# A transformer layer on one core: a new order for the last attention group and the batch norm sums, and a shorter form of its last two tiles

## The reference, cut to what matters

```python
h = layernorm(x)
q, k, v = relu(h @ Wq + bq), relu(h @ Wk + bk), relu(h @ Wv + bv)
y = softmax(q @ k.T / sqrt(512) - 1e4 * causal) @ v
x1 = x + layernorm(relu(y @ Wo + bo))
h2 = layernorm(x1)
for side in (out, in_):                     # two sides, each with its own weights
    xc = einsum('ngf,gf->ng', h2.reshape(n, 128, 4), conv_w) + conv_b
    mean, var = over all 8192 rows of xc    # batch norm: needs every row
    xa = gelu((xc - mean) * rsqrt(var + eps) * gamma + beta)
    score[side] = softmax(xa @ lin_w.T + lin_b)
# out: (h2 @ W) kept where score is in its top 32 of 512 columns, times the score
# in:  (h2 kept where score is in its top 32, times the score) @ W
return x1 + layernorm(out_branch + in_branch + bias)
```

## Time and profile before

| what | value |
|---|---|
| median of 3 runs | 2086.85 us (2084.85 to 2088.97) |
| the profiled execution, its own time | 2083.91 us |
| its span, first to last instruction | 2082.1 us |
| TensorE (PE) busy | 2008.6 us, 96% |
| VectorE (DVE) busy | 1529.4 us, 73% |
| ScalarE (ACT) busy | 1104.9 us, 53% |
| GpSimd (POOL) busy | 1096.3 us, 53% |
| mean granted TensorE clock | 0.992 of full |

### The profile page before, as it was taken

One profiled execution on the slowest core, in us unless ns is written; L12 is line 12 of the kernel. 1 busy time (PEld: TensorE's weight loads), 2 busy tenths in 40 slices (PEclk: granted clock), 3 DMA queues, 4 the chain that ended last, 5 costly groups with the idle time before them and its releaser, 6 DMA issues. The chain is left out here.

```text
span 2082.1 us, 30834 instructions
## 1 busy us (share of the span) xinstructions
PE 2008.6 (96%) x9402; PEld 940.9 (45%) x9402; DVE 1529.4 (73%) x3344; ACT 1104.9 (53%) x2270; POOL 1096.3 (53%) x1302
## 2 busy tenths in 40 slices
PE   8999999999999999999999999988999999999997
PEld 4444444444444444444444444443444444444443
DVE  6676554677645568655557764578999999999998
ACT  5444333254333344442334433325888888888886
POOL 2243322363332254423234431324899999999998
PEclk9999999999999999999999999989999999999999
DMA  5344343354242424434334332451222222222322
GB/s 184 79 91 106 75 96 73 103 115 117 69 107 65 110 69 117 104 83 99 76 95 111 93 87 60 115 152 41 69 94 98 86 87 97 87 90 93 102 77 71
DMA packets 301593, 194.85 MB, mean 94 GB/s; under 512 B 223858, under 2 KB 241394, under 8 KB 301428
## 3 DMA queue, kind: packets, MB, share of 16 engines
q1 hardware_dynamic: 301428, 192.88, 34.8%
HBM read 82.69 MB, written 58.72 MB: 68 GB/s over the span
## 5 line engine op out<-in xcount | busy, mean ns | idle before, releaser
L616 PE MATMUL psum<-hT,w_hi 128*128 128x512 f16 (+1 forms) x1544 | 458.4, 379 | 0.0
L616 PE MATMUL psum<-kT,qT 128*128 128x512 f16 (+3 forms) x1920 | 363.4, 347 | 1.5 <-DVE kT L1112 1.5
L616 PE MATMUL psum<-v,pT 128*128 128x512 f16 x1632 | 362.5, 379 | 0.6 <-DMA pT<-phl 0.6
L616 PE MATMUL psum<-hT,w_lo 128*128 128x512 f16 (+1 forms) x772 | 292.3, 379 | 0.0
L616 PEld LDWEIGHTS psum<-kT,qT 128*128 128x128 f16 x1920 | 180.9, 98 | 184.3 <-issue 2.9
L868 ACT ACTIVATE sS<-sS,nm 128x128 f32<-128x128 f32 (+7 forms) x64 | 76.9, 1202 | 348.0 <-DVE nm L1149 347.8
L857 ACT ACTIVATE raw<-psum,bqkv_s 128x512 f32<-128x512 f32 x192 | 131.2, 683 | 218.8 <-PE psum L616 216.8
L616 PEld LDWEIGHTS psum<-v,pT 128*128 128x128 f16 x1632 | 159.7, 98 | 193.0 <-issue 1.1
L1373 DVE MAX8 c<-cut 128x8 f32<-128x512 f32 x384 | 244.2, 676 | 0.0
L616 PEld LDWEIGHTS psum<-hT,w_hi 128*128 128x128 f16 x1544 | 151.5, 98 | 176.1 <-DVE w_lo L1086 0.2
L1498 POOL TENSOR_SCALAR ve<-mv 128x1 f32<-128x1 f32 x64 | 21.9, 342 | 347.1 <-DVE mv L1175 346.2
(11 more groups left out here) (159 smaller groups left out, 3819.1 us busy)
## 6 DMA issues: line engine op xcount, KB each, us to landing
xg<-x SPq DMA_DIRECT2D x64, 256.0 KB, 5.3
xr<-x SPq DMA_DIRECT2D x64, 256.0 KB, 2.9
x_scratch<-xr SPq DMA_DIRECT2D x64, 256.0 KB, 2.1
h_scratch<-hb SPq DMA_DIRECT2D x64, 256.0 KB, 3.0
h<-h_scratch SPq DMA_DIRECT2D x64, 256.0 KB, 2.7
x<-x_scratch SPq DMA_DIRECT2D x64, 256.0 KB, 2.9
out<-zn SPq DMA_DIRECT2D x59, 256.0 KB, 2.0
xc_scratch<-dsq SPq DMA_DIRECT2D x64, 128.0 KB, 2.0
```

The lines of the kernel that those rows point to most:

```text
L616: mm = nc.tensor.matmul(outp, stat(a), mov(c), start=(n == 0 and k == 0), stop=(n == total - 1 and k == 2))
```

## The change

It touches what lies after the scores of tile 63. Four parts:

1. The lists of all engines for the last four tiles are written out by hand in another order, and the main loops end one half step earlier (PREP + 4).
2. For the tiles 62 and 63 (`SHORT` = 62 on), VectorE makes the sum x + scale*o in one step without the layer norm's shift (`residual_in`); it takes statistics of that, and convolves rows that are centred but not yet scaled (`unscaled_convolution`), the scale coming in with the pilot's subtraction (`scaled_deviations`). ScalarE adds the shift afterwards, for the copy of x1 that is stored (`residual_out`). `normed` and GpSimd's `residual` fall away for these two tiles; h2 for the store is made later, by `second_rows`.
3. TensorE's sums of tiles 60 to 62 come straight after its last product; the transposes of the first columns after that, between pieces of `keep_warm` (4, 8, 8 and 6 matmuls, where there were 8 and 12) that wait for steps of tile 63. VectorE makes the last three steps of the batch norm in place of GpSimd.
4. The first gelu is made a side at a time over all four tiles (it was: both sides of one tile, then of the other three), the logits and exponentials of tile 0 likewise. The bias matmuls of both sides come before the first wait for a gelu, and the transposes of the second group come before the logits of tile 1.

```diff
 (TensorE)
+                earlier_sums()
+                for T in range(OWN, TS - 1):
+                    tile_sums(T)
+                keep_warm(4)
                 pe.wait_ge(o_ev.sem, o_ev.at(TS - 1))
-                pe.wait_ge(fw_lo, C)
                 conv_columns(0)
-                channel_sums()
-                keep_warm(12)
+                pe.wait_ge(rsd2_ok.sem, rsd2_ok.at(TS - 1))
+                keep_warm(8)
+                pe.wait_ge(pr_ok.sem, pr_ok.at(2 * (TS - 1) + 1))
+                keep_warm(8)
+                tile_sums(TS - 1)
+                keep_warm(6)
...
-                logits(0)
+                first_logits()
                 pe.wait_ge(fw_lo, C)
+                conv_columns(1)
 (ScalarE)
+                def residual_out(T):
+                    act.wait_ge(xin_ok.sem, xin_ok.at(T - SHORT))
+                    act.wait_ge(rs2_ok.sem, rs2_ok.at(T))
+                    nc.scalar.activation(ob[:, T % 2, :], xr[:, T % 4, :], ACT.Identity, bias=rs2[:, T % 2, 1:2])
...
+                normed(TS - 3)
+                exponential(TS - 1)
+                hi_p(TS - 1, first)
+                hi_p(TS - 1, rest_of)
+                nc.scalar.activation(warm[:, 0:1], expo[:, 0:1], ACT.Gelu)
                 for T in (TS - 2, TS - 1):
                     relu_o(T)
-                    normed(T)
-                nc.scalar.activation(warm[:, 0:1], expo[:, 0:1], ACT.Gelu)
+                    residual_out(T)
 (VectorE)
+                def residual_in(T):
+                    dve.wait_ge(rsd2_ok.sem, rsd2_ok.at(T))
+                    dve.wait_ge(xr_in[T % 4].sem, xr_in[T % 4].at(T // 4))
+                    nc.vector.scalar_tensor_tensor(xr[:, T % 4, :], ob[:, T % 2, :], rs2[:, T % 2, 0:1], xr[:, T % 4, :],
+                                                   ALU.mult, ALU.add).then_inc(xin_ok.sem, 1)
...
-                convolution(TS - 4)
-                residual_stats(TS - 3)
-                bias_o(TS - 2)
-                attention_stats(TS - 2)
-                convolution(TS - 3)
-                residual_stats(TS - 2)
-                bias_o(TS - 1)
-                attention_stats(TS - 1)
-                convolution(TS - 2)
-                residual_stats(TS - 1)
-                convolution(TS - 1)
+                T = TS - 1
+                attention_stats(T - 2)
+                score_chunk(T, 0)
...
+                score_chunk(T, 3)
+                score_max(T)
+                deviations(T - 3)
+                residual_stats(T - 2)
+                weight_in_lo(0)
+                lo_p(T, first)
+                lo_p(T, rest_of)
+                convolution(T - 2)
+                bias_o(T - 1)
+                deviations(T - 2)
+                attention_stats(T - 1)
+                weight_in_lo(1)
+                residual_in(T - 1)
+                shifted_stats(T - 1)
+                unscaled_convolution(T - 1)
+                scaled_deviations(T - 1)
+                weight_in_lo(2)
+                bias_o(T)
+                attention_stats(T)
+                second_rows(T - 1)
+                residual_in(T)
+                shifted_stats(T)
+                unscaled_convolution(T)
+                scaled_deviations(T)
+                second_rows(T)
 (SyncE)
+                load_residual(TS - 2)
+                store_x1(TS - 4)
+                store_xc(TS - 5)
+                load_residual(TS - 1)
+                store_h2(TS - 4)
+                store_xc(TS - 4)
+                store_x1(TS - 3)
                 transpose_p(TS - 1)
-                load_residual(TS - 1)
-                store_x1(TS - 3)
+                store_h2(TS - 3)
+                store_xc(TS - 3)
```

More of the change, by code:

```diff
@@ L436, in gelu_at @@
         def gelu_at(n):
[L438 removed]
+            return n // GROUP + 1
         def live(i, lag):
@@ L545, in _ @@
                 sp.dma_start(cw_b[:], convw).then_inc(cw_in, 16)
-                for H in range(PREP + 5):
+                for H in range(PREP + 4):
                     g, h = divmod(H, HALF)
@@ L968, in gelu, with first_exponentials @@
                     for s in range(2):
-                        i = nc.scalar.activation(xa[:, slot, j0:j1, s, :], X_BANKS[:, j0:j1, s, :], ACT.Gelu, bias=bn_bi[:, s:s + 1],
+                        i = nc.scalar.activation(xa[:, slot, :, s, :], X_BANKS[:, :, s, :], ACT.Gelu, bias=bn_bi[:, s:s + 1],
                                                  scale=bn_sc[:, s:s + 1])
                     i.then_inc(gelu_ok.sem, 1)
+                def first_exponentials():
+                    for s in range(2):
+                        act.wait_ge(mx_ok.sem, mx_ok.at(s))
+                        nc.scalar.activation(nmx[:, s:s + 1], m8[:, s, 0:1], ACT.Copy, scale=-1.0).then_inc(nmx_ok.sem, 1)
+                        act.wait_ge(nmx_ok.sem, nmx_ok.at(s))
+                        nc.scalar.activation(e8[:, s, :], m8[:, s, :], ACT.Exp, bias=nmx[:, s:s + 1])
+                        nc.scalar.activation(ex[:, 0, s, :], L_BANK[s], ACT.Exp, bias=nmx[:, s:s + 1],
+                                             accum_out=den[:, 0, s:s + 1]).then_inc(ex_ok.sem, 1)
                 def exponentials(n):
```

196 lines of the change are left out of this document (122 added, 74 removed).

## The result

The changed kernel took 2075.11 us in the median of 4 runs (2074.09 to 2075.72), the kernel before, run beside it and with its earlier runs, 2085.85 (2084.46 to 2088.97). The ratio is 0.9949, with a 95% interval of 0.9936 to 0.9961: 0.5% faster, a gain of 10.7 us by the medians. The prediction had 2080.0 and a range of 2075.5 to 2085.0.

A forecast was written before the change was run, and what follows sets the result against it. TensorE bounds up to 1384.93 us, VectorE from 1415.01, with a 30.1 us passage between. Savings of 5.3, 0.25 and 1.3 sum to 6.85, say 6.8; from the 2086.85 median, 2080.0 us, range 2075.5 to 2085.0.

The forecast's parts named there:

- The last product: Scores up to tile 63's last product: row maximum about 0.6 us later, absorbed by slack; cost 0, ends 0 and +2 us.
- Sums, wait and tile 63: Last product to `bn_dev`: a new wait of some 3.7 us, bias 2.1 us later, shorter tile 63 steps; -5.3 us in all.
- Batch norm: Batch norm's power to gelu: last steps on VectorE instead of GpSimd save 0.25 us, ends 0 and -0.4.
- A side at a time: Gelu to first MAX8: gelu, logits and exponentials of tile 0 by side take 5.9 us instead of 7.18, -1.3 us.
- Clock: TensorE's clock falls during or soon after the one-column sums; idle matmuls restore it, the second eight taking 1.8 us.
- The step that failed: Claim that the VectorE-bound branch stage has no slack, so the end comes earlier by whatever the 30.1 us passage loses.
- The passage: Stretch between the stages, from tile 63's last product to VectorE's first MAX8 without notable wait; 30.1 us neither stage can use.
- the rival that makes it *slower: TensorE stays at half clock into the branch stage, each such tile holding VectorE up by 8 us; 2096 us, chance 0.03.

The follow-up runs named there:

- the second profile: The changed kernel run again without any change, to get another profile; that execution took 2073.67 us.
- the first pair of profiles: The first profiled executions of the kernel before and of the changed kernel, nothing else changed: 2083.91 and 2075.72 us.
- b_order: Changed kernel with tile 62's columns in a buffer of their own and tile 63's bias ahead of a weight row; ratio 0.9931 to the kernel before.
- b_mix: b_order plus idle matmuls between the one-column sums, tile 62's sums behind the transposes, fewer fill-ins before tile 63's sums; median 2071.12 us.

## Why the prediction was wrong, point by point

*The last product.* "I cost this at 0", ends 0 and +2. It ended 0.84 us later in the profile. In the eleven profiles that have the new order it ends up to 1.8 us after 1384.93, 0.7 in the mean. The cost was real, since the row maximum came 1.8 us later, not 0.6: VectorE waits 1.71 us there for a store of columns, which the step didn't count. In the second profile the same wait is 0.99 us, the maximum 0.9 later and the product on time, so the slack was about 0.9, not 0.6.

*Sums, wait and tile 63.* "-5.3", from 20.45 to 15.2 (with the product where it was). Measured 14.67, so -5.8 from the product, and -4.94 by the clock time of `bn_dev`. The wait, its place on the path, the bias later (2.3 us for 2.1) and the length of tile 63's steps each came within 0.5 us. The term is all short form (6.1 us behind the bias by its run, some 1.9 of it clock); the order contributes nothing by itself, which the prediction left together in one sum.

*Batch norm.* "-0.25"; -0.35 in the profiles.

*A side at a time.* "-1.3"; -1.33. The rule of the Trainium skill ("ScalarE: Activation LUTs", section "What ACT_TABLE_LOAD costs"), by which a drain of about 1380 ns follows the load, would have made this part 0; the row decided, and the runs with and without the part bear the row out.

*Clock.* "at full clock they take 8 x 0.23 = 1.8 us". They took 1.90, and the sums behind them 1.06. The second eight had the full clock, as forecast, and the fall came where it was looked for (1388.6). The run without fill-ins and the one with fill-ins between the sums show it from both sides: one-column sums fill TensorE's time in the trace, and the clock falls all the same. The Trainium skill ("TensorE: Matmul & The Clock Gate", section "What's actually happening") has activity release the throttle; with busy time read as activity, the run with tile 62's own place, in which the clock falls to 0.50 at 1388 with TensorE full since the last product, speaks against it.

*The step that failed* stands in the first paragraph: "Whatever it loses, the end comes earlier by, since the VectorE-bound stage behind it holds no slack in which it could be lost." It looked for slack in which a gain is lost, and found none; what the change does in that stage was put at 0, since VectorE was taken to set its length alone. The passage lost 7.5 us by the first pair of profiles, 6.6 by the clock time with the late product, which is what had been forecast (6.85). The rest came in the stage taken as fixed:

- its first tiles run beside a TensorE that is partly at half clock, and lose 0.76 us before in one profile and 2.3 in the other; the changed kernel, with half clock there too but with TensorE's work begun 2.7 us sooner, loses nothing. The prediction had this mechanism only as the rival that makes it *slower*, with 0.03, and had judged it from the mean clock of 600 us that begin at 1450, behind the place where it happens;
- its later holds and its end are set by GpSimd's lag, not by VectorE: 0.8 us of the first pair, 2.7 of the second. The earlier trace rows has VectorE at 599.30 of 600 us, but its period is so near to GpSimd's that busy shares can't tell which leads, and the chain of the profile's page named POOL with 16% and DVE with 6%. It was read for the passage only.

That 6.6 lies so near 6.85 is in part luck: the passage itself gave 0.6 more than forecast, and the late product, put at 0, took 0.84 back.

The range was carried down to 2075.5 "for runs in which the passage before was slower". That happens (8.05 in place of 7.18 at the logits), but the larger part of the difference between runs of before, 2.3 of 3.2 us, is in the stage behind. The forecast also took the profiled execution, the fastest of before's first five, as the model of the others.

## What to carry to other kernels

Where the profile shows an engine full, ask the chain of waits who sets the end of that stage before calling it fixed: here an engine at 94% with a period 0.05 us longer than that of the full one set its last microseconds, and taking 0.26 us a tile from it shortened the stage by 1.3 to 2.5 us. A passage with light work on TensorE costs twice, where the clock falls and in the first tiles behind it; wide idle matmuls, put between the small ones or into a tile with little work, bought 2.5 us in each of two places (12.82 to 10.32 in the passage, and the run of before with twelve more). And one profile of a kernel whose runs spread by 5 us isn't the kernel: take a second before you build a sum of terms under 1 us on it.

## What the runs showed of the hardware

- Eight records of one-column float32 matmuls (the four sums of a tile) take 0.95 to 1.06 us at a granted clock of 1.00 and 1.84 to 1.87 at 0.50. Thirty-two of them, one behind another right after full work, saw the clock fall while they ran (b_order). With four 512-column matmuls behind each of the first three eights, and the last eight behind the transposes, it stayed at 1.00 (b_mix).
- The same program has the clock fall at other times in other executions: between 1404 and 1441 it is at 0.50 from 1414.0 to 1417.4, 1424.3 to 1427.7 and 1434.5 to 1437.9 in one profile of before, and from 1406.1 to 1409.5, 1416.3 to 1419.8, 1423.2 to 1430.0 and 1436.8 to 1440.2 in the next. The second is 3.2 us longer.
- On GpSimd a 128x1 step takes 0.19 us, but with the wait for the step ahead of it it cost 0.26 of the period (from the start of the power to the next large step 0.77 us with it, 0.51 without).
